# Dividing 128-column float products into two 64-column halves of the TensorE array in a recall block

## The chip, the cores and the metric

The program runs on one core of a Trainium2 chip. The metric is the device time of one execution in microseconds (us); the number compared is the median of several executions. The kernel uses five engines of the core: TensorE (PE, with its weight loads listed apart as PEld), VectorE (DVE), ScalarE (ACT), GpSimd (POOL) and SyncE (SP, here only DMA queues). Each engine works through its own instructions in order, and they wait for one another by semaphores.

## The reference

The program computes five layers over 8 batches of 1,056 tokens of 64 numbers: a patch embedding, an attention layer, a mixture of 16 experts, a recurrent "recall" layer and a mixture of 8 experts. The change touches the fourth alone. Cut to what matters it is, for every batch and token:

```python
def step(carry, v_prev):                       # v_prev: the token's 64 numbers; n = 256
    x_state, rho = carry
    x_t = 0.97 * x_state + relu(v_prev @ Dx.T)
    x_t = x_t / max(sum(abs(x_t)), 1e-12)
    a_star = einsum('bdn,bn->bd', rho, x_t)
    y_t = relu(_ln(a_star) @ Dy.T) * relu(x_t)
    v_star = _ln(y_t @ E.T)
    rho_t = 0.97 * rho + _ln(v_prev)[:, :, None] * x_t[:, None, :]
    return (x_t, rho_t), v_star
```

All of it is float32.

## The kernel before, in words

The recurrence is computed in tiles of 128 tokens: 8 full tiles and one of 32 for each batch. The block is `recall_answer_block`; `x_all` holds x with its 256 numbers along the partitions in two halves (`f` = 0, 1), tokens along the row. One loop counter n = 9 b + t runs through batch b and tile t on every engine (n from 0 to 89; the last 18 are the tail for what lags behind). What PE does in iteration n, in this order:

- `score(n+1)` (L2247): the 128x128 products of x with itself within a tile, two float products (one for each f) with 128 result columns, into `p_s`. VectorE multiplies it by the decay triangle (`mask`, L2426) into `pm`.
- `turn_x` (L2254): two transposes that bring x's tile to tokens-on-partitions; ScalarE copies them to `xr` (L2356).
- from batch 2 on, for the batch two back: `core` (L2300, 352 result columns, once in each of iterations 1 to 6), whose result VectorE turns into `yT` (`gate`, L2434; the next `core` waits for the gate before it); in iterations 7 and 8 `answer` (L2309), ten and eight products with 64 result columns.
- for the batch one back, in iterations 7, 8 and 0, `turn_la` (L2291): three transposes of the normalised rows `la`, which VectorE makes by `la_centre` (L2453) in iteration 5 and `la_scale` (L2460) in iteration 6.
- `weigh(n)`: the masked scores times the values (L2270, one product) and, from the second tile on, x times the state (L2274, two products), each with 64 result columns. It waits for `mask(n)` and for the state's copy.
- `keep_state` (L2282): two products with 64 result columns add the tile to the state in `p_r`; ScalarE copies it out (L2360).

Every float product stands in the trace as two pairs of a weight load and a matmul. VectorE runs, besides masks and gates, the scans of x for later batches (L1850, two for each batch: in iterations 4 and 6 of batch 0, in 4 and 7 of batch 1, and from then on in iteration 8 and in iteration 0 of the next batch), and the row statistics (L2440, L2445, L2148, L2156). GpSimd computes the inverse roots and adds the answer to `hid` (L2132 to L2140, about 8 us a batch). The block ends when all engines are through; the last piece there is GpSimd's L2140, and then the second expert stage starts, in which PE is the chain that sets the end.

In the tail (n from 72 on) the last two batches' `turn_la`, `core` and `answer` run, mixed with the routing (top-k) of the first batch of the next stage on VectorE.

Of the kernel before, what the change touches and what calls it, by code (L numbers as in the profile page):

```python
# [20 lines left out]
P = 128  # L21
B, C, T, V, D = 8, 64, 128, 64, 64
# [6 lines left out]
FULL = SEQ // P  # L29
CH = SEQ // 3  # L30
# [2128 lines left out]
def recall_answer_block(g, x_all, vn_all, rate_scr, feed, kb, trio, own, steps):  # L2159

    nc, hid, arg = g.nc, g.hid, g.arg
# [6 lines left out]
    la_turned, laT_ready, cored, gated, answered = (g.sem("k_" + n) for n in ("la_turned", "laT_ready", "cored", "gated", "answered"))  # L2168
    v_step = kb["v_step"]
    with ExitStack() as c:  # L2170
        sb = lambda n, s, d=F32: c.enter_context(nc.sbuf_tensor("k_" + n, s, d))
        ps = lambda n, s: c.enter_context(nc.psum_tensor("k_" + n, s, F32))
        tri, fade, pm, xr, state, a_sb, la, laT, yT, v_sb, dyT, eT = (
            kb[n] for n in ("tri", "fade", "pm", "xr", "state", "a_sb", "la", "laT", "yT", "v_sb", "dyT", "eT"))
# [5 lines left out]
        p_s, p_w = ps("p_s", [P, 2, 512]), ps("p_w", [P, 2, 512])  # L2180
        p_t, p_r = p_w[:, 0, :], p_w[:, 1, :]
# [4 lines left out]
        core_bank = lambda b, k: p_s[:, 0, :] if b >= B - 2 and k % 2 else p_y  # L2186
        AFTER = NT * B
        block = c.enter_context(nc.Block())
        rows_of = lambda t: P if t < FULL else TXT
        span = lambda t: slice(t * P, t * P + rows_of(t))  # L2190
        wide = lambda m: m.to_broadcast([P, NT, D])

        @block.sync
        def _(sp):
            _, load_biases, spread_out, spread_in, _ = sync_steps(sp)
            load_biases()
            load_levels(g, sp, kb, EARLY, B, late["scaled"], 1)
            send_rates(g, sp, kb, rate_scr, EARLY, B, 1)
            for b in range(EARLY, B):
                spread_rate(sp, kb, rate_scr, b)  # L2200
            sp.wait_ge(weighed, NT * 6)
            sp.wait_ge(gated, KW * 6)
            spread_out(0)
            spread_in(0, range(NC))
# [32 lines left out]
        @block.tensor  # L2237
        def _(pe):
            def score(n):
                b, t = divmod(n, NT)  # L2240
                if n >= 2:
                    pe.wait_ge(masked, n - 1)
                if t == 0:
                    pe.wait_ge(scanned, 2 * b + 2)
                x, rows = x_all[:, b, :, :], rows_of(t)
                for f in range(2):
                    last = nc.tensor.matmul(p_s[0:rows, n % 2, 0:rows], x[:, f, span(t)], x[:, f, span(t)], start=(f == 0), stop=(f == 1))  # L2247
                last.then_inc(scored, 1)

            def turn_x(b, t):  # L2250
                m = FULL * b + t
                pe.wait_ge(x_rows, m)
                for f in range(2):
                    last = nc.tensor.transpose(p_t[:, f * P:f * P + P], x_all[:, b, f, span(t)], g.eye[:])  # L2254
                last.then_inc(x_turned, 1)

            def weigh(n):
                b, t = divmod(n, NT)
                rows = rows_of(t)
                if t == 0:  # L2260
                    pe.wait_ge(a_kept, 2 * b)
                if n == FULL:
                    pe.wait_ge(kb["level"], LEVEL_STEPS + NC)
                    pe.wait_ge(kb["copied"], 2)
                if t == FULL:
                    pe.wait_ge(a_kept, 2 * b)
                    pe.wait_ge(v_kept, 2 * max(b - 2, 0))
                out = p_a[:, t, :] if t < FULL else p_last[0:TXT, 0:D]
                pe.wait_ge(masked, n + 1)
                last = nc.tensor.matmul(out, pm[0:rows, n % 2, 0:rows], vn_all[0:rows, b, t, :], start=True, stop=(t == 0))  # L2270
                if t:
                    pe.wait_ge(held, FULL * b + t)
                    for f in range(2):
                        last = nc.tensor.matmul(out, x_all[:, b, f, span(t)], state[:, f, :], start=False, stop=(f == 1))  # L2274
                last.then_inc(weighed, 1)

            def keep_state(b, t):
                m = FULL * b + t
                pe.wait_ge(x_rows, m + 1)
                pe.wait_ge(held, m)  # L2280
                for f in range(2):
                    last = nc.tensor.matmul(p_r[:, f * D:f * D + D], xr[:, m % 2, f * P:f * P + P], vn_all[:, b, t, :],  # L2282
                                            start=(t == 0 and f == 0), stop=(t == FULL - 1), skip_group_check=True)
                last.then_inc(stated, 1)

            def turn_la(b, k):
                pe.wait_ge(la_step, 2 * b + 2)
                pe.wait_ge(laT_ready, 3 * b + k)
                pe.wait_ge(gated, KW * b)
                for t in range(3 * k, 3 * k + 3):  # L2290
                    last = nc.tensor.transpose(p_y[0:D, t % 3 * P:t % 3 * P + P], la[:, t, :], g.eye[:])  # L2291
                last.then_inc(la_turned, 1)

            def core(b, k):
                f, a = divmod(k, NC)
                pe.wait_ge(laT_ready, 3 * b + 3)
                pe.wait_ge(gated, KW * b + (k if b < B - 2 else max(k - 1, 0)))
                if b >= B - 2:
                    pe.wait_ge(masked, NT * B)
                nc.tensor.matmul(core_bank(b, k)[:, 0:CH], dyT[:, f, :], laT[:, a * CH:a * CH + CH], start=True, stop=True).then_inc(cored, 1)  # L2300

            def answer(b, half):
                pe.wait_ge(gated, KW * b + KW)
                pe.wait_ge(v_kept, 2 * b)
                pe.wait_ge(a_kept, 2 * min(b + 2, B))
                for t in ((0, 1, 2, 3, 4), (5, 6, 7, 8))[half]:
                    out = p_v[:, t, :] if t < FULL else p_last[:, D:2 * D]
                    for f in range(2):
                        last = nc.tensor.matmul(out, yT[:, f, t * P:t * P + P], eT[:, f, :], start=(f == 0), stop=(f == 1))  # L2309
                last.then_inc(answered, 1)  # L2310

            _, turn_tokens, logits, turn_gates, _ = tensor_steps(pe)
            score(0)
            turn_x(0, 0)
            for n in range(NT * (B + 2)):
                b, t = divmod(n, NT)
                if n + 1 < NT * B:
                    score(n + 1)
                    if t + 1 != FULL:
                        turn_x(*divmod(n + 1, NT))  # L2320
                if n == 0:
                    pe.wait_ge(set_up, 4)
                    pe.wait_ge(own["w_copied"], 3)
                if b == B and t == 7:
                    for half in range(2):
                        answer(b - 2, half)
                if 1 <= b <= B and t >= 7:
                    turn_la(b - 1, t - 7)
                if b >= 2 and t == 0:
                    turn_la(b - 2, 2)  # L2330
                if n == AFTER + 8:
                    turn_gates(0)
                if b >= 2 and 1 <= t <= KW:
                    core(b - 2, t - 1)
                if b >= 2 and t >= 7 and b != B:
                    answer(b - 2, t - 7)
                if b < B:
                    weigh(n)
                    if t < FULL:
                        keep_state(b, t)  # L2340
                if AFTER + 2 <= n <= AFTER + 3:
                    if n == AFTER + 2:
                        pe.wait_ge(x_rows, FULL * B)
                        pe.wait_ge(held, FULL * B)
                    turn_tokens(0, n - AFTER - 2)
                if n == AFTER + 4:
                    logits(0)
# [195 lines left out]
def all_stages(g):  # L2543

    nc, arg = g.nc, g.arg
    with ExitStack() as c:
# [41 lines left out]
        with ExitStack() as c3:  # L2588
            buffers = recall_buffers(g, c3, c)
            trio = c3.enter_context(nc.psum_tensor("k_trio", [P, 3, 512], F32))  # L2590
            drive_block(g, x_all, feed, rate_scr, buffers, trio, own, steps)
            recall_answer_block(g, x_all, vn_all, rate_scr, feed, buffers, trio, own, steps)
# [39 lines left out]
```

## Time and profile before

| | us |
|---|---|
| median of 3 executions | 1810.58 |
| lowest, highest | 1808.53, 1818.72 |
| the profiled execution | 1824.75 |
| its span in the trace | 1822.9 |
| the recall block within it | 1325 to 1543 |
| PE busy, VectorE busy (whole span) | 1691.1, 1258.9 |
| granted TensorE clock, mean | 0.943 |

The trace is of one execution, some 14 us longer than the median. Busy times are unions of an engine's instructions, and the mean length of a matmul includes the time in which it drains, so the rate of PE is read from the distance between the starts of groups and not from the lengths. PEclk is the granted share of TensorE's full clock of 2.4 GHz; 0.50 is the lower level, 1.2 GHz.

### The profile page before, as it was taken

What the parts mean: (1) busy time and instruction counts of PE and PEld (TensorE: products, weight loads), DVE (VectorE), ACT (ScalarE), POOL (GpSimd) and SP (SyncE); (2) the same over time, 40 slices, a digit from 0 to 9 for tenths busy, and PEclk for the clock granted to TensorE, in tenths of its full rate; (3) what the DMA queues carried; (4) which work ended last, traced back from release to release, by engine and by line L of the source; (5) the groups of instructions that cost most, each with busy time, mean ns of one, the idle gap of its engine ahead of it and who ended that gap; (6) DMA issues with size and microseconds to landing.
All of it is one profiled execution on the core that took longest, in us unless ns stands there. A gap on an engine that the chain in (4) does not pass through costs nothing. (4 is left out here: it accounts for less than half of the span.)

```text
span 1822.9 us, 50042 instructions
## 1 busy us (share of the span) xinstructions
PE 1691.1 (93%) x20010; PEld 820.6 (45%) x20010; DVE 1258.9 (69%) x3153; ACT 1041.5 (57%) x1963; POOL 348.3 (19%) x325
## 2 busy tenths in 40 slices
PE   7978999999999999999999999999899997999999
PEld 3331222222222222222223655657488995566667
DVE  3459888888888888888722688886776664444432
ACT  1330777777777777777655555555533332666654
POOL 3212000000000000000100146655304434110000
PEclk9965999999999999999866999999999997999999
DMA  5741012121212112110113875563120002253350
GB/s 206 267 100 33 8 37 50 36 51 37 50 31 51 37 40 47 33 37 15 36 37 81 161 149 111 100 126 70 43 74 13 1 2 49 57 98 63 63 98 20
DMA packets 89587, 119.37 MB, mean 65 GB/s; under 512 B 31340, under 2 KB 72374, under 8 KB 87310
## 3 DMA queue, kind: packets, MB, share of 16 engines
q1 hardware_dynamic: 84874, 107.28, 27.0%
q0 software_dynamic: 2992, 8.44, 1.2%
q8 instruction: 161, 2.64, 0.6%
q10 hardware_dynamic: 1492, 0.46, 0.1%
q14 instruction: 68, 0.56, 0.1%
HBM read 97.29 MB, written 18.86 MB: 64 GB/s over the span
## 5 line engine op out<-in xcount | busy, mean ns | idle before, releaser
L870 ACT ACTIVATE b_prob<-b_p_s 128x512 f32<-128x512 f32 x1104 | 570.5, 599 | 273.8 <-PE b_p_s L1060 255.2
L893 DVE TENSOR_REDUCE b_m<-b_p_m 128x1 f32<-128x1024 f32 x512 | 604.0, 1219 | 85.1 <-PE b_p_s L1060 64.9
L1088 PE MATMUL b_p_o<-b_prob,v_all 128*9 128x512 f32 x2304 | 314.7, 630 | 1.0
L1486 ACT ACTIVATE d_hidden<-d_p_z 128x704 f32<-128x704 f32 x192 | 135.1, 755 | 98.6 <-PE d_p_z L1386 96.6
L1060 PE MATMUL b_p_s<-b_q,b_k 51*64 51x512 bf16 x1024 | 183.0, 420 | 2.4 <-ACT b_prob L870 2.4
L1486 ACT ACTIVATE n_hidden<-n_p_z 128x704 f32<-128x704 f32 x192 | 135.1, 755 | 84.6 <-PE n_p_z L1386 82.3
L1001 PE MATMUL b_p_m<-b_qk 48*64 48x512 bf16 x856 | 162.7, 441 | 21.8 <-ACT b_prob L870 5.4
L1060 PE MATMUL b_p_s<-b_qk 51*64 51x512 bf16 x1024 | 177.5, 401 | 2.2 <-ACT b_prob L870 2.2
L848 POOL DMA_DIRECT2D sum_scr<-b_sums x46 | 25.3, 550 | 718.5 <-ACT b_sums L860 631.8
L1402 PE MATMUL d_p_y<-d_hidden,d_w 64*64 64x352 f32 x1536 | 143.1, 460 | 9.0 <-DVE d_yT L1604 8.9
L1001 PE MATMUL b_p_m<-b_k,b_q 48*64 48x512 bf16 x800 | 137.2, 392 | 12.2 <-ACT b_prob L870 6.5
L1402 PE MATMUL n_p_y<-n_hidden,n_w 64*64 64x352 f32 x1536 | 142.1, 460 | 0.1
L1001 PEld LDWEIGHTS b_p_m<-b_qk 48*64 48x64 bf16 x856 | 38.4, 111 | 188.0 <-DVE b_m L893 123.2
L1001 PEld LDWEIGHTS b_p_m<-b_k,b_q 48*64 48x64 bf16 x800 | 35.1, 104 | 164.4 <-DVE b_m L893 98.6
L1402 PEld LDWEIGHTS d_p_y<-d_hidden,d_w 64*64 64x64 f32 x1536 | 74.3, 133 | 47.1 <-DVE d_yT L1604 19.2
L1386 PE MATMUL d_p_z<-d_xg,d_w 64*64 64x352 f32 x1024 | 94.0, 465 | 0.5 <-issue 0.5
L1386 PE MATMUL n_p_z<-n_xg,n_w 64*64 64x352 f32 x1024 | 92.6, 466 | 0.0
L1402 PEld LDWEIGHTS n_p_y<-n_hidden,n_w 64*64 64x64 f32 x1536 | 72.2, 133 | 39.8 <-DVE n_yT L1604 10.0
L1619 DVE TENSOR_TENSOR d_xg<-d_xd,d_c_wide 128x352 f32<-128x352 f32 x84 | 50.8, 648 | 47.6 <-PEq L674 31.8
L1604 DVE TENSOR_TENSOR n_yT<-n_yT,n_p_y 128x352 f32<-128x352 f32 x24 | 12.5, 522 | 95.0 <-ACT n_yT L1493 95.0
L1088 PEld LDWEIGHTS b_p_o<-b_prob,v_all 128*9 128x9 f32 x2304 | 37.7, 89 | 83.0 <-issue 54.9
L1001 PE MATMUL b_p_m<-b_k_head,b_q_head 48*64 48x512 bf16 x392 | 67.0, 405 | 6.3 <-ACT b_prob L870 4.6
(391 smaller groups left out, 2599.7 us busy)
## 6 DMA issues: line engine op xcount, KB each, us to landing
d_c_wide<-d_c_scr SPq DMA_DIRECT2D x40, 704.0 KB, 12.1
m_x_all<-n_c_scr SPq DMA_DIRECT2D x48, 352.0 KB, 7.9
xt<-in_x SPq DMA_DIRECT2D x16, 1024.0 KB, 10.6
sum_scr<-b_sums POOLq DMA_DIRECT2D x31, 256.0 KB, 2.4
qk_scr<-a_qk_part SPq DMA_DIRECT2D x24, 256.0 KB, 3.0
b_qk<-d_c_scr SPq DMA_DIRECT2D x8, 704.0 KB, 18.2
k_rate<-rate_scr SPq DMA_DIRECT2D x8, 528.0 KB, 4.4
b_qk<-qk_scr SPq DMA_DIRECT2D x56, 66.0 KB
```

The costliest lines, as they stand in the source:

```text
L848: pool.dma_start(g.sum_scr[b, p, :, a * WIDE:a * WIDE + w], sums[:, n % 2, 0:w]).then_inc(sum_sent[n % 2], 16)
L870: nc.scalar.activation(prob[:, U % PR_RING, 0:w], p_s[:, U % S_RING, 0:w], ACT.Exp, scale=float(D) ** -0.5).then_inc(exp_done, 1)
L893: nc.vector.tensor_reduce(m3[:, x, 0:1], p_m[:, s, :, :].rearrange("p k n -> p (k n)"), axis=AX.X, op=ALU.max).then_inc(rows_free, 1)
L1001: last = nc.tensor.matmul(out[e:e + 64, k, :], q[:, t * P + e:t * P + e + 64], keys[:, k * WIDE:k * WIDE + WIDE], start=True, stop=True)
L1060: last = nc.tensor.matmul(out[e:e + 64, :], k_st[s][r, q, jt * P + e:jt * P + e + 64], q_st[s][r, q, a * WIDE:a * WIDE + WIDE], start=True ...
L1088: last = nc.tensor.matmul(p_o[32 * i:32 * i + DH + 1, :], v[:, jt, p * QUAD + i, :], prob[:, slot, :], start=(jt == 0), stop=(jt == TILES[ ...
L1386: last = nc.tensor.matmul(own["p_z"][h * D:h * D + D, n % 2, q, 0:CH], w1[r, pr, cols:cols + D], own["xg"][n // HALVES % XR][r, :], start= ...
L1402: last = nc.tensor.matmul(own["p_y"][q * D:q * D + D, h, 0:CH], w2[r, 2 * pr + q, f, :], own["hidden"][r, n % HR, q, :], start=(k == 0), s ...
L1486: nc.scalar.activation(own["hidden"][:, n % HR, :, :], own["p_z"][:, n % 2, :, 0:CH], ACT.Relu).then_inc(relu_done, 1)
L1604: nc.vector.tensor_tensor(own["yT"][:, cols], own["yT"][:, cols], own["p_y"][:, 1, 0:CH], ALU.add).then_inc(sum_copied, 1)
L1619: nc.vector.tensor_tensor(own["xg"][j % XR], own["xd"][b % 3][:, a * CH:a * CH + CH], own["c_wide"][b % 2][a][:, pr, :], ALU.mult)\
```

## The change

Every float product whose weights have 128 columns is issued as two products of 64 weight columns, one for each column half of the array (result partitions 0 to 63 and 64 to 127), with the same moving data. The two transposes of `turn_x` become products with the identity, divided in the same way. The moving data, the waits and the increments stay; the increment is on the last product of the group. The small products of the 32-token tile and the transposes of `turn_la` are not divided.

```diff
+        halves_of = lambda rows: [(0, D), (D, P)] if rows == P else [(0, rows)]
...
                 for f in range(2):
-                    last = nc.tensor.matmul(p_s[0:rows, n % 2, 0:rows], x[:, f, span(t)], x[:, f, span(t)], start=(f == 0), stop=(f == 1))
+                    for lo, hi in halves_of(rows):
+                        last = nc.tensor.matmul(p_s[lo:hi, n % 2, 0:rows], x[:, f, t * P + lo:t * P + hi], x[:, f, span(t)], start=(f == 0), stop=(f == 1),
+                                                skip_group_check=True)
...
                 for f in range(2):
-                    last = nc.tensor.transpose(p_t[:, f * P:f * P + P], x_all[:, b, f, span(t)], g.eye[:])
+                    for lo, hi in halves_of(P):
+                        last = nc.tensor.matmul(p_t[lo:hi, f * P:f * P + P], x_all[:, b, f, t * P + lo:t * P + hi], g.eye[:, :], start=True, stop=True,
+                                                skip_group_check=True)
...
-                last = nc.tensor.matmul(out, pm[0:rows, n % 2, 0:rows], vn_all[0:rows, b, t, :], start=True, stop=(t == 0))
+                for lo, hi in halves_of(rows):
+                    last = nc.tensor.matmul(out[lo:hi, :], pm[0:rows, n % 2, lo:hi], vn_all[0:rows, b, t, :], start=True, stop=(t == 0), skip_group_check=True)
...
                     for f in range(2):
-                        last = nc.tensor.matmul(out, x_all[:, b, f, span(t)], state[:, f, :], start=False, stop=(f == 1))
+                        for lo, hi in halves_of(rows):
+                            last = nc.tensor.matmul(out[lo:hi, :], x_all[:, b, f, t * P + lo:t * P + hi], state[:, f, :], start=False, stop=(f == 1),
+                                                    skip_group_check=True)
...
                 for f in range(2):
-                    last = nc.tensor.matmul(p_r[:, f * D:f * D + D], xr[:, m % 2, f * P:f * P + P], vn_all[:, b, t, :],
-                                            start=(t == 0 and f == 0), stop=(t == FULL - 1), skip_group_check=True)
+                    for lo, hi in halves_of(P):
+                        last = nc.tensor.matmul(p_r[lo:hi, f * D:f * D + D], xr[:, m % 2, f * P + lo:f * P + hi], vn_all[:, b, t, :],
+                                                start=(t == 0 and f == 0), stop=(t == FULL - 1), skip_group_check=True)
...
-                nc.tensor.matmul(core_bank(b, k)[:, 0:CH], dyT[:, f, :], laT[:, a * CH:a * CH + CH], start=True, stop=True).then_inc(cored, 1)
+                for lo, hi in halves_of(P):
+                    last = nc.tensor.matmul(core_bank(b, k)[lo:hi, 0:CH], dyT[:, f, lo:hi], laT[:, a * CH:a * CH + CH], start=True, stop=True,
+                                            skip_group_check=True)
+                last.then_inc(cored, 1)
...
                     for f in range(2):
-                        last = nc.tensor.matmul(out, yT[:, f, t * P:t * P + P], eT[:, f, :], start=(f == 0), stop=(f == 1))
+                        for lo, hi in halves_of(P):
+                            last = nc.tensor.matmul(out[lo:hi, :], yT[:, f, t * P + lo:t * P + hi], eT[:, f, :], start=(f == 0), stop=(f == 1),
+                                                    skip_group_check=True)
```

## Rows read from the trace of the kernel before

**Rows 1.** The page: busy time of PE and VectorE over the span.
```profile
PE   1691.1 (93%) x20010; PEld 820.6 (45%) x20010; DVE 1258.9 (69%) x3153; ACT 1041.5 (57%) x1963; POOL 348.3 (19%) x325
...
PE 15%; DVE 0%; issue 0%; POOL 0%; POOLq 0%
```

**Rows 2.** Windows: stretch, its length, busy PE, PEld, DVE, ACT, POOL, PEclk, DMA.
```profile
1330.20:1340.40 10.20, 9.90 (x88) 9.56 (x88) 10.01 (x11) 3.41 (x11) 0.00 (x0) 1.00 0.08 14
1340.40:1354.60 14.20, 14.20 (x130) 13.74 (x130) 8.42 (x34) 5.79 (x18) 2.02 (x2) 1.00 0.31 117
1354.60:1365.50 10.90, 8.86 (x70) 7.74 (x71) 9.72 (x23) 4.39 (x13) 0.00 (x0) 1.00 0.24 78
1365.50:1380.20 14.70, 13.74 (x111) 12.51 (x109) 10.06 (x54) 3.36 (x10) 7.16 (x9) 1.00 0.05 19
...
1404.25:1414.93 10.68, 10.19 (x84) 9.31 (x84) 8.58 (x21) 4.41 (x13) 6.17 (x4) 1.00 0.01 2
1414.93:1428.40 13.47, 13.47 (x110) 12.46 (x109) 7.61 (x36) 3.35 (x10) 3.55 (x4) 1.00 0.01 1
...
1476.70:1503.60 26.90, 26.90 (x224) 25.08 (x223) 15.15 (x86) 8.88 (x26) 11.93 (x14) 1.00 0.01 2
...
1516.90:1524.50 7.60, 7.56 (x36) 7.56 (x37) 3.05 (x14) 0.00 (x0) 5.53 (x5) 0.50 0.01 2
```

**Rows 3.** Timeline of PE: a steady step, and one answer (start, length, group).
```profile
1446.20 0.33 PE L2270 MATMUL k_p_a<-v_all,k_pm 128*128 128x64 f32 x2
1446.37 0.61 PE L2274 MATMUL k_p_a<-k_state,m_x_all 128*128 128x64 f32 x4
1446.81 0.61 PE L2282 MATMUL k_p_w<-v_all,k_xr 128*128 128x64 f32 x4
1447.26 0.66 PE L2247 MATMUL k_p_s<-m_x_all 128*128 128x128 f32 x4
1447.76 0.38 PE L2254 MATMUL k_p_w<-eye,m_x_all 128*128 128x128 f32 x2
1447.98 0.76 PE L2300 MATMUL k_trio<-k_laT,k_dyT 128*128 128x352 f32 x2
1448.57 0.33 PE L2270 MATMUL k_p_a<-v_all,k_pm 128*128 128x64 f32 x2
...
1454.71 1.90 PE L2309 MATMUL k_trio<-k_eT,k_yT 128*128 128x64 f32 x16
1456.54 0.29 PE L2270 MATMUL k_trio<-v_all,k_pm 32*32 32x64 f32 x2
```

**Rows 4.** PE in tiles elsewhere: timeline of the expert stage; the page's attention group.
```profile
1590.81 0.64 PE L1374 MATMUL n_p_w<-eye,n_yT 64*64 64x64 f32 x31
1591.28 0.46 PE L1386 MATMUL n_p_z<-n_w_raw,n_w 64*64 64x352 f32 x1
...
L1088 PE MATMUL b_p_o<-b_prob,v_all 128*9 128x512 f32 x2304 | 314.7, 630 | 1.0
```

**Rows 5.** Timeline: VectorE's chain around a batch's first tiles, and the core behind it.
```profile
1454.37 0.29 DVE L2426 TENSOR_TENSOR k_pm<-k_p_s,k_tri 128x128 f32<-128x128 f32 x1 [3.50 <-PE k_p_s L2247]
1454.58 3.17 DVE L1850 TENSOR_TENSOR_SCAN m_x_all<-m_x_all,k_rate 128x1056 f32<-128x1056 f32 x1
...
1461.91 0.51 DVE L2434 SCALAR_TENSOR_TENSOR k_yT<-k_trio,m_x_all 128x352 f32<-128x352 f32 x1
...
1462.57 0.83 PE L2300 MATMUL k_trio<-k_laT,k_dyT 128*128 128x352 f32 x2 [0.49 <-DVE k_yT L2434]
```

**Rows 6.** Timeline: `la_scale` on VectorE and `turn_la` on PE.
```profile
1449.21 0.75 DVE L2460 TENSOR_TENSOR k_la<-k_la,k_a_mv 128x576 f32<-128x576 f32 x1
...
1450.02 0.52 PE L2291 MATMUL k_trio<-eye,k_la 128*64 128x128 f32 x3
```

**Rows 7.** Timeline of the tail: the long answer, and GpSimd's last addition.
```profile
1516.94 7.95 PE L2309 MATMUL k_trio<-k_eT,k_yT 128*128 128x64 f32 x36 [4.89 <-DVE k_yT L2434]
...
1541.67 1.40 POOL L2140 TENSOR_TENSOR hid<-hid,k_v_sb 128x576 f32<-128x576 f32 x1
```

## The prediction

> **What bounds the kernel now.** I read the page first. PE is busy for 93% of the span and makes nearly all of the chain that ended last [rows 1], but a busy PE says little, because its matmuls overlap. So I went to the windows of the recall block, cut at the tiles of the loop [rows 2]. The reader is to see two kinds of stretch. From tile 2 to tile 7 of a batch (13.47 us) PE never idles while VectorE is at 7.61: PE sets the pace. From tile 7 to tile 2 of the next batch (10.68 us) PE is busy 10.19, and VectorE, with two scans, 8.58: there both are near their limit. The two make a batch of 24.15 us. Batches 0 and 1 have stretches in which VectorE fills 10.01 of 10.20 and 9.72 of 10.90 us.
>
> Then the timeline of one PE step [rows 3]: 1446.20 to 1448.57, 2.37 us. Its 2 + 4 + 4 records with 64 result columns start 0.111 us apart (four of L2282 in 0.45), and so do the two transposes (0.22). The core's two records with 352 columns take 0.295 each, 0.84 ns a column. By that rate 64 columns would stream in 0.054, so the 64-column records are not bound by streaming but by loading 128 weight columns, 0.111 each. Score, with 128 columns, streams in 0.107: load and stream are level.
>
> **The change, part by part.** What decides is the price of a 64-column load and matmul when the other half of the array works beside it. The nearest row is the expert stage, which uses four 64x64 tiles: between 1590.81 and 1591.28 it starts 32 float records of 64 result columns (31 in the group, one beside it), 0.47 / 8 = 0.059 us for four [rows 4]. Two of those tiles share the same rows and differ in the column half; were their loads one after the other, a round would need twice 0.056, the half of 0.111. For all 128 rows the trace shows column tiles in the attention: 2,304 records of 512 columns in 314.7 us of busy time, 0.137 each, where 512 columns at 0.84 ns stream in 0.43: three to four run side by side. So I take 0.059 for one record on each half.
>
> A rule speaks against that. Loads overlap there only across row groups, and two column halves of a 128-row product share theirs: the Trainium skill, "TensorE: Matmul & The Clock Gate", Part 3 (packing small matmuls), says that a load overlaps with in-flight matmuls only when the row group differs. The trace disagrees for the expert stage's column halves, by the 0.059 above, and shows nothing for halves of 128 rows with 64-column loads. By the rule the sum below would be a loss (first rival).
>
> - A product with 64 result columns is two records now, 0.222, and then four on two halves, 2 x 0.059 = 0.117: it saves 0.105. Bounds: 0 if loads queue (4 x 0.056), 0.115 if only streaming counts.
> - Score: 4 records of 0.111 become 8, two at a time, 4 x 0.107 to 0.111: nothing. It lies on PE's own path, so if the halves did not overlap it would cost 0.43.
> - Core: 2 x 0.295 become 4, two at a time: nothing; 0.59 if they did not overlap, which the attention row makes unlikely.
> - turn_x: two transposes of one record each, 0.22, become eight records of 128 columns, 4 x 0.111 = 0.44: it costs 0.22. Bounds 0.21 to 0.64, the latter if the halves do not overlap.
> - No wait is added. The increments stay on the last product of each group.
>
> A full step has five short products and one turn: 5 x 0.105 - 0.22 = 0.30 saved of 2.37. An answer tile has two: 0.21. Were PE the bound everywhere, a batch would save 56 x 0.105 - 8 x 0.22 = 4.1 us, and eight batches 33. But not all of it is PE's.
>
> Steady batch, tile 7 to tile 2. VectorE runs one unbroken chain here: the mask at 1454.37 starts when the first score of the next batch is there, then come scan, statistics, mask, scan, statistics, mask and the gate of 1461.91, and the second core waits 0.49 for that gate [rows 5]. From mask to core, 8.2 us, nothing gets faster. Only what precedes the mask does: weigh and keep of tile 7, 0.53. So 0.53 is saved here, where PE alone would give 1.3 and the 0.49.
>
> Tile 2 to tile 7. Four full steps save 1.2. In the last interval weigh, keep and the five-tile answer save 0.53 + 1.05. But turn_la waits for la_scale, which ends at 1449.96, and starts at 1450.02 [rows 6]: no slack. la_scale stands behind the gate of the last core, and PE then reaches turn_la 0.53 sooner after that core. So I take 0.5 off: 1.1. Together 2.3.
>
> What I checked behind these: the state's copy (L2360, 0.28) has score, turn, core and the first weigh as cover, 1.6 us; a core follows the last by 2.06, while core and gate need about 1.4; VectorE would be busy 16.2 of 21.3 us a batch.
>
> | stretch | saved, us |
> |---|---|
> | 1325 to 1330, two steps, partly waiting for VectorE | 0.5 |
> | 1330.2 to 1340.4, VectorE full | 0 |
> | 1340.4 to 1354.6: PE-bound, -2.2, less 0.6 hidden by a scan | 1.6 |
> | 1354.6 to 1365.5, scans, VectorE chain | 0 |
> | 1365.5 to 1380.2: three steps 0.9, last interval 1.1 | 2.0 |
> | 1380.2 to 1390.8 | 0.5 |
> | three steady batches to 1463.2, 0.53 + 2.3 each | 8.4 |
> | 1463.2 to 1476.7 | 2.3 |
> | 1476.7 to 1503.6: no scans; intervals 1.15 - 0.2 + 0.1 + 5 x 0.30 + 1.1 + 1.37, less 0.3 as VectorE has routing work | 4.7 |
> | the long answer of the tail | 3.4 |
> | the last answer | 0 |
>
> The long answer [rows 7] runs at a granted clock of 0.50 [rows 2], the 1.2 GHz level, after PE sat idle for VectorE's routing: 36 records take 7.6 us. In halves at the same clock: 18 products x 2 x 0.117 = 4.2. It is on the path: turn_la and the six cores of batch 7 follow, then their gates, then GpSimd's 6 us, which end the block at 1543.1. The last answer (1536.4 to 1540.6) lies beside GpSimd's work, so its 2 us are hidden.
>
> Sum: 23.4 us. The stages behind the block are bound by PE and start when it ends, so they shift. Against the profiled execution's 1824.75 us that is 1801.4; the same 23.4 off the median of 1810.58 gives 1787.2.
>
> **The rivals.**
>
> *Loads of the two halves queue* (the other side). If the halves of 128 rows load one after the other, a short product needs 4 x 0.056 = 0.22 as now, and turn_x still costs 0.22 on 64 tiles. Some 50 of the 64 lie where PE sets the pace: +11 us, 1822. It decides as soon as a short product saves less than 64 x 0.22 / 448 = 0.032 us. For it: with 128 rows the trace has column tiles only with loads of 9 columns, so nothing there shows a 64-column load beside another. Against it: the four-tile row, in which two column halves share rows. This is what the page's rule comes to.
>
> *Half an overlap.* A round of 0.085 instead of 0.059 gives 0.05 a short product: 22 - 14 = 8 us on PE, and some of it where VectorE binds: 4 to 8 us, 1804 to 1806.
>
> *VectorE takes it.* If its in-order queue (masks behind scans, statistics and la_centre) binds in the 13.47 us stretch too, four steps save half and the tail's answer alone is safe: 12 to 15 us, 1797. For it: at 21 us a batch VectorE is at 76%, and several of its chains had slack below 1 us. Against: in each step it now idles 0.9 us in two waits.
>
> *The clock comes back sooner.* The half clock now lasts from about 1514 to 1534. With halves the long answer streams without pause; if the clock rises before the transposes and cores, these get up to 3 us shorter, and 6 us in all: 1783. The transfers of `m_x_all`, which run until about 1542 and start behind the same answer, let no more through.
>
> **How the numbers follow.** A measurement of this kernel tells a change from none at about 0.5%, 9 us. Forecast as summed (1780 to 1795): 0.58. Clock sooner or nearer to the full 33 us (1774 to 1780): 0.09. VectorE (1795 to 1801): 0.13. Half an overlap: 0.10. Loads queue: 0.10. Faster by over 0.5% (below 1801.5): the first three, 0.80; within: half an overlap, 0.10; slower: 0.10. The range of 1778 to 1805 takes in the bounds of the main case, VectorE and most of the half overlap, and leaves out the loss and the best end; the main case's own is 1780 to 1795.
>
> **What would show it.** In the new timeline: eight records of L2282 between group starts 0.23 apart (0.45 if loads queue, and turn_x at 0.44 either way); a steady step of 2.06; batches of 21.3 us with PE waiting about 1.3 us for the gate in tile 1 and 0.5 for la_scale before turn_la; the long answer 4.2 us long. If the steps are right and the sum is not, the next place is VectorE's chains. What would break it outright: a gap on PE at each change between full and 32-token tiles that is now hidden, or the two halves of a full-height product not running together.

## The result, and the profile after

The changed kernel takes 1791.84 us (median of 4, 1780.75 to 1795.65), the kernel before in the same rounds 1814.38 (median of 4, 1808.53 to 1818.72): a ratio of 0.9874, interval 0.984 to 0.9907. Forecast were 1787 us (1778 to 1805) and a ratio of 1787.2 / 1810.58 = 0.987; the kernel before had itself moved from 1810.58 to 1814.38 with the fourth execution. The profiled execution took 1795.65 us, its span 1793.8.

Single executions of one kernel differ by about 1%, and much of that arises ahead of the recall block, where no code differs. So kernels are compared by **the block**: from the start of the first score's first matmul to the start of the first matmul of the next stage (L1336). It began at 1325.0 before and at 1320.4 after; what follows it takes 279.3 and 280.2 us. Between, it took 218.60 us before and 193.27 after: 25.3 saved, where the prediction's sum was 23.4.

The page of the kernel after, busy times, and the two groups of the expert stage's chain that still end last; against [rows 1] PE has 1,632 more records and 39 us less of busy time, 32 of it in the block (202.12 us before).

```profile
PE 1652.3 (92%) x21642; PEld 780.3 (43%) x21642; DVE 1249.6 (70%) x3153; ACT 1041.6 (58%) x1963; POOL 355.6 (20%) x325
...
PE n_p_z L1386 7%; PE n_p_y L1402 7%; PE n_p_w L1336 1%; PE n_p_w L1374 0%; PE n_p_w L1345 0%; PE n_p_y L1365 0%; PE n_p_z L1415 0%; DVE hid L1593 0%; PE n_p_w L1354 0%; PE n_p_w L1355 0%; POOL n_yT L1306 0%; POOLq L2170 0%
```

The windows after (columns as in [rows 2]): the whole block; then the stretches that were 14.70, 13.47, 10.68 and 26.90 long [rows 2]; last the long answer, 7.60 before.

```profile
1320.40:1513.67 193.27, 170.14 (x3198) 140.46 (x3198) 135.74 (x561) 68.01 (x194) 87.95 (x72) 0.97 0.13 34
...
1359.93:1371.78 11.85, 11.10 (x230) 9.52 (x227) 8.90 (x52) 3.36 (x10) 7.24 (x7) 1.00 0.07 21
...
1402.19:1413.53 11.34, 10.88 (x230) 9.52 (x227) 7.30 (x36) 3.35 (x10) 2.89 (x4) 1.00 0.01 3
1413.53:1423.33 9.80, 9.23 (x175) 7.48 (x173) 8.32 (x21) 4.53 (x13) 8.77 (x4) 1.00 0.01 3
...
1455.80:1478.37 22.57, 22.10 (x456) 18.57 (x452) 14.07 (x80) 9.00 (x26) 10.62 (x12) 1.00 0.01 4
...
1491.98:1496.02 4.04, 4.04 (x73) 3.92 (x73) 3.01 (x14) 0.00 (x0) 2.24 (x2) 0.50 0.01 4
```

A steady batch went from 24.15 to 11.34 + 9.80 = 21.14 us. The window that was 26.90 long ends 0.20 behind the last tile's first product, so 22.57 is to be set against 26.70. The long answer has twice the records, and from its first to its last start it takes 3.79 instead of 7.52 us, at the same granted clock of 0.50.

The timeline of PE after: a steady step, then the end of interval 6, interval 7, and the core in tile 1.

```profile
1427.42 0.31 PE L2276 MATMUL k_p_a<-v_all,k_pm 128*64 128x64 f32 x4
1427.54 0.43 PE L2281 MATMUL k_p_a<-k_state,m_x_all 128*64 128x64 f32 x8
1427.77 0.43 PE L2291 MATMUL k_p_w<-v_all,k_xr 128*64 128x64 f32 x8
1428.01 0.64 PE L2249 MATMUL k_p_s<-m_x_all 128*64 128x128 f32 x8
1428.44 0.64 PE L2258 MATMUL k_p_w<-eye,m_x_all 128*64 128x128 f32 x8
1428.88 0.79 PE L2310 MATMUL k_trio<-k_laT,k_dyT 128*64 128x352 f32 x4
1429.47 0.31 PE L2276 MATMUL k_p_a<-v_all,k_pm 128*64 128x64 f32 x4
...
1433.00 0.52 PE L2300 MATMUL k_trio<-eye,k_la 128*64 128x128 f32 x3 [0.46 <-DVE k_la L2474]
1433.45 1.39 PE L2322 MATMUL k_trio<-k_eT,k_yT 128*64 128x64 f32 x40
...
1435.69 0.61 PE L2258 MATMUL k_p_w<-eye,m_x_all 128*64 128x128 f32 x8
1436.23 0.52 PE L2300 MATMUL k_trio<-eye,k_la 128*64 128x128 f32 x3
1436.67 1.15 PE L2322 MATMUL k_trio<-k_eT,k_yT 128*64 128x64 f32 x32
1437.75 0.29 PE L2276 MATMUL k_trio<-v_all,k_pm 32*32 32x64 f32 x2
...
1443.85 0.81 PE L2310 MATMUL k_trio<-k_laT,k_dyT 128*64 128x352 f32 x4 [0.57 <-DVE k_yT L2448]
```

Start to start, the eight records of L2281 take 0.23 us where four took 0.44, score 0.43 (0.50 before), the turn 0.44 (0.22 before), the core 0.59 as before: 2.05 for the step, against 2.37 [rows 3]. (Line numbers moved with the edit: `score` is L2249, `turn_x` L2258, `weigh` L2276 and L2281, `keep_state` L2291, `turn_la` L2300, `core` L2310, `answer` L2322.) PE now waits at two places of a batch, 0.46 for `la_scale` and 0.57 for a gate.

The timeline of VectorE after, in the same batch (against [rows 5, 6]):

```profile
1432.20 0.75 DVE L2474 TENSOR_TENSOR k_la<-k_la,k_a_mv 128x576 f32<-128x576 f32 x1
...
1435.91 0.29 DVE L2440 TENSOR_TENSOR k_pm<-k_p_s,k_tri 128x128 f32<-128x128 f32 x1 [2.26 <-PE k_p_s L2249]
1436.11 3.17 DVE L1850 TENSOR_TENSOR_SCAN m_x_all<-m_x_all,k_rate 128x1056 f32<-128x1056 f32 x1
...
1439.89 2.57 DVE L1850 TENSOR_TENSOR_SCAN m_x_all<-m_x_all,k_rate 128x1056 f32<-128x1056 f32 x1
...
1443.20 0.51 DVE L2448 SCALAR_TENSOR_TENSOR k_yT<-k_trio,m_x_all 128x352 f32<-128x352 f32 x1
```

### The profile page after: what moved, and what is told of

Same layout as the page of the kernel before. It is cut to its first block and busy times, and to the rows that moved or that the text cites. A ratio compares the mean times of both kernels' runs of the same rounds, so it can differ in the third digit from the quotient of the medians.

```text
span 1793.8 us, 53306 instructions
## 1 busy us (share of the span) xinstructions
PE 1652.3 (92%) x21642; PEld 780.3 (43%) x21642; DVE 1249.6 (70%) x3153; ACT 1041.6 (58%) x1963; POOL 355.6 (20%) x325
## 5 line engine op out<-in xcount | busy, mean ns | idle before, releaser
L1088 PE MATMUL b_p_o<-b_prob,v_all 128*9 128x512 f32 x2304 | 310.9, 623 | 1.0
L1001 PE MATMUL b_p_m<-b_qk 48*64 48x512 bf16 x856 | 162.7, 442 | 21.8 <-ACT b_prob L870 5.4
L848 POOL DMA_DIRECT2D sum_scr<-b_sums x46 | 25.3, 550 | 718.4 <-ACT b_sums L860 696.8
```

The lines of the kernel that those rows point to most:

```text
L848: pool.dma_start(g.sum_scr[b, p, :, a * WIDE:a * WIDE + w], sums[:, n % 2, 0:w]).then_inc(sum_sent[n % 2], 16)
L1001: last = nc.tensor.matmul(out[e:e + 64, k, :], q[:, t * P + e:t * P + e + 64], keys[:, k * WIDE:k * WIDE + WIDE], start=True, stop=True)
L1088: last = nc.tensor.matmul(p_o[32 * i:32 * i + DH + 1, :], v[:, jt, p * QUAD + i, :], prob[:, slot, :], start=(jt == 0), stop=(jt == TILES[ ...
```

## The experiments

Blocks are read from each kernel's own trace. A step is one interval with a core and no wait; a batch is a steady one; the tail runs from the long answer's start to the next stage.

| kernel | block | step | batch | tail |
|---|---|---|---|---|
| before | 218.6 | 2.37 | 24.15 | 26.7 |
| after | 193.3 | 2.05 | 21.14 | 21.7 |
| e3, one half left out | 191.8 | 2.05 | 21.12 | 21.9 |
| e4, one half twice | 227.3 | 2.63 | 26.33 | 22.8 |
| e5, halves in the outer loop | 193.0 | 2.05 | 21.15 | 21.8 |
| e1, transposes kept | 194.9 | 2.13 | 21.48 | 22.7 |
| e8, score and core whole | 219.7 | 2.75 | 24.97 | 22.9 |
| e9, only short products divided | 195.9 | 2.19 | 21.71 | 20.8 |
| e6, only the turn divided | 246.7 | 2.94 | 27.79 | 26.3 |
| e7, `la_scale` ahead of the gate | 188.8 | 2.05 | 19.82 | 20.1 |
| e10, e7 and statistics later | 189.3 | 2.05 | 19.82 | 21.5 |
| e12, GpSimd's wide pieces narrow | 185.4 | 2.05 | 20.36 | 16.8 |
| e11, only the long answer divided | 214.0 | 2.37 | 24.15 | 21.7 |

Each experiment but e10 was executed once, so it is judged by its trace. A block is good to about 1 us: from its start to the first tile of batch 1 after, e3, e7, e10 and e12 run the same code, and this takes 18.2, 17.5, 19.5, 19.3 and 17.5 us. Steps and batches repeat to 0.02 where the work is the same.

### Do the halves run side by side? (e3, e4, e5)

In e3 and e4 the short products (those with 64 result columns) of the full tiles, from batch 1 on, use another list of halves: e3 leaves the upper half out, e4 computes the lower one twice, so neither has the upper half's results. e5 only changes the order.

```diff
+        short_of = lambda rows, b: halves_of(rows) if b == 0 or rows != P else [(0, D)]              # e3
+        short_of = lambda rows, b: halves_of(rows) if b == 0 or rows != P else [(0, D), (0, D)]      # e4
...
-                for f in range(2):
-                    for lo, hi in halves_of(rows):
+                for lo, hi in halves_of(rows):                                                       # e5
+                    for f in range(2):
```

> Leaves out, from batch 1 on, the upper half (result partitions 64 to 127) of every product with 64 result columns (weigh, keep_state, answer); score, core and turn_x are as in the changed kernel. Theory (the two halves load and work side by side, a round of two costs what one costs, 0.058 us): PE's steps do not change, a steady step stays at 2.05 us, and the block from the first score to the first matmul of the next stage stays at 193 us, within 2. Rival (the halves share something, and a half alone would be quicker than 0.058 a record): a short product falls below 0.117, a step below 2.0, and the block to 185 or less.

> From batch 1 on, the upper half of every product with 64 result columns is replaced by a second copy of the lower one, so the same number of records all go to one column half (the upper half's results are not computed). This makes the rival of the prediction, loads that queue, by construction. Theory: four records one after the other, 4 x 0.058 = 0.23 us a short product, so a steady step is 2.05 + 5 x 0.117 = 2.64 us, the long answer of the tail goes from 4.1 to 8.2 us, and the block from 193 to 230 to 240 us. Rival (what counts is the number of records or their issue, not where they go): step and block as in the changed kernel, 2.05 and 193 us.

> The changed kernel with the order turned round: both products (f = 0, 1) of the lower half are issued first, then both of the upper half, in score, turn_x, weigh's state part, keep_state and answer. The same work, four records to one half in a row instead of two. Theory 1 (matmuls start in program order, so two records overlap only where the half changes): a group of eight records takes some 6 to 7 rounds where it took 4, a steady step is 2.5 to 2.9 us instead of 2.05, the block 215 us or more. Theory 2 (each half has its own queue and the order is free): 2.05 and 193 us.

The timeline of PE in e3, then in e4:

```profile
1419.84 0.28 PE L2277 MATMUL k_p_a<-v_all,k_pm 128*64 128x64 f32 x2
1419.96 0.40 PE L2282 MATMUL k_p_a<-k_state,m_x_all 128*64 128x64 f32 x4
```

```profile
1449.81 0.39 PE L2277 MATMUL k_p_a<-v_all,k_pm 128*64 128x64 f32 x4
1450.04 0.63 PE L2282 MATMUL k_p_a<-k_state,m_x_all 128*64 128x64 f32 x8
1450.51 0.57 PE L2292 MATMUL k_p_w<-v_all,k_xr 128*64 128x64 f32 x7
1450.86 0.32 PE L2250 MATMUL k_p_s<-m_x_all 128*64 128x128 f32 x1
1450.92 0.22 PE L2292 MATMUL k_p_w<-v_all,k_xr 128*64 128x64 f32 x1
```

With half the records e3's groups start as far apart as after, 0.12 for the first: the second half is free. (Of the 1.4 us by which its block is shorter, 1.3 lie ahead of tile 7 of batch 1, where blocks vary by chance.) With the same number of records, all on one half, e4's take 0.23 and 0.47, and its block is 227.3 us, 9 slower than before: it is the first rival, built. (That is less than the 230 to 240 expected; the step, 2.63, is as expected, the long answer takes 6.27 from first to last start and not 8.2.) So the number of records costs nothing as long as they are spread over both halves: which half each goes to decides. e5 puts two records of one half in a row in every divided group but the first and the core, and neither step nor block moves: the order within a group doesn't matter. In e4 the records even start out of order: the first record of `score` (L2250, 1450.86) starts ahead of the last of `keep_state` (L2292, 1450.92), which is issued before it. The trace doesn't name the halves, but in e4 only the upper one has nothing in line before `score`. Each half is served as if it had its own queue.

For halves of 128 rows a pair of loads takes 0.058 us, where one after the other takes 0.117, as in e4. The rule that the prediction weighed ("TensorE: Matmul & The Clock Gate", Part 3, in the Trainium skill: loads overlap only across row groups) doesn't hold there. The Trainium skill's "TensorEngine Tiling (Array Packing)", Key Properties, says that different tiles can load and multiply in parallel, and e3 agrees.

### What the parts that gain nothing are for (e1, e8, e9, e6)

e1 takes back the turn alone; e8 score and core; e9 all three, so that only the short products are divided; e6 is the kernel before with only the turn divided.

```diff
# e1, e9
-                    for lo, hi in halves_of(P):
-                        last = nc.tensor.matmul(p_t[lo:hi, f * P:f * P + P], x_all[:, b, f, t * P + lo:t * P + hi], g.eye[:, :], start=True, stop=True,
-                                                skip_group_check=True)
+                    last = nc.tensor.transpose(p_t[:, f * P:f * P + P], x_all[:, b, f, span(t)], g.eye[:])
# e8, e9 (the core likewise)
-                    for lo, hi in halves_of(rows):
-                        last = nc.tensor.matmul(p_s[lo:hi, n % 2, 0:rows], x[:, f, t * P + lo:t * P + hi], x[:, f, span(t)], start=(f == 0), stop=(f == 1),
-                                                skip_group_check=True)
+                    last = nc.tensor.matmul(p_s[0:rows, n % 2, 0:rows], x[:, f, span(t)], x[:, f, span(t)], start=(f == 0), stop=(f == 1))
```

> The changed kernel, but turn_x is again two transposes with 128 weight columns. Theory 1 (a change between weights of 128 and of 64 columns is free, so only the 0.22 us of the turn counts): a steady step falls from 2.05 to 1.83 us, a batch from 21.1 to about 19.9 (the VectorE chain keeps its part), the block from 193 to 185 us. Theory 2 (the array drains at each change of width, as its loads can't be taken ahead): two changes a step cost 0.1 to 0.2 us each, and the step is 2.0 to 2.2 us, the block 190 to 197 us; gaps then stand before the load of turn_x and the load behind it.

> The changed kernel, but score and core are again single products with 128 weight columns; weigh, keep_state, turn_x and answer stay in halves. By streaming alone nothing is gained or lost by dividing these two. Theory 1 (each change of width costs 0.15): four changes a step instead of none, a steady step of 2.05 + 0.6 = 2.65 us, the block 222 to 230 us. Theory 2 (the change of width costs only beside transposes): 2.05 and 193 us.

> Only the products with 64 result columns (weigh, keep_state, answer) are in halves; score, turn_x (as transposes) and core keep 128 weight columns, as in the kernel before. A step has two changes of width, since score, turn and core follow one another. By 0.15 to 0.175 each: 2.37 - 0.53 + 0.30 to 0.35 = 2.14 to 2.19 us a steady step, the block about 197 us. Rival (changes of width cost only beside transposes or only in the four-change kernel's order): 1.83 us and 185.

> The kernel before, with turn_x alone changed (products with the identity, in halves); all other products keep 128 weight columns. Theory: the turn costs 0.22 us more, and each of its two changes of width about 0.15 (the whole-transposes run showed 0.30 for two), so a steady step goes from 2.37 to 2.9 us and the block from 218.6 to about 242 us. Rival (the turn alone counts): 2.59 us and 229.

The weight loads of e1 around the transposes, and the timeline of PE in e8, one step:

```profile
1441.07 0.45 PEld L2249 LDWEIGHTS k_p_s<-m_x_all 128*64 128x64 f32 x8
1441.69 0.20 PEld L2257 LDWEIGHTS k_p_w<-eye,m_x_all 128*128 128x128 f32 x2 [0.17 <-issue]
1442.06 0.20 PEld L2308 LDWEIGHTS k_trio<-k_laT,k_dyT 128*64 128x64 f32 x4 [0.17 <-issue]
```

```profile
1452.46 0.40 PE L2289 MATMUL k_p_w<-v_all,k_xr 128*64 128x64 f32 x8
1452.79 0.71 PE L2248 MATMUL k_p_s<-m_x_all 128*128 128x128 f32 x4
1453.43 0.66 PE L2256 MATMUL k_p_w<-eye,m_x_all 128*64 128x128 f32 x8
1454.02 0.86 PE L2307 MATMUL k_trio<-k_laT,k_dyT 128*128 128x352 f32 x2
1454.81 0.34 PE L2274 MATMUL k_p_a<-v_all,k_pm 128*64 128x64 f32 x4
```

In e1 each passage between products in halves and whole ones leaves the load side idle for 0.17 us. e1 has two in a step: its turn is 0.22 shorter and its step 0.08 longer, so the two cost 0.30, 0.15 each. e8 has four: 2.75 against 2.05, 0.175 each. e9 has two: by the prediction's terms 2.37 - 5 x 0.105 = 1.845 and 2.19 is measured, 0.17 each. e6 has two as well: 2.37 + 0.22 leaves 0.35. With four passages e8 loses the whole gain (219.7 us, below the 222 to 230 expected, though its step is longer than the 2.65 expected). e6, whose turn is by itself only 0.22 dearer, is 28 us slower than before (246.7 us where 242 was expected). Dividing score, turn and core, which save nothing of their own, is what keeps the step free of passages; between e9 and after that is worth 0.14 a step and 2.6 us of block. It is the smaller part: e9, with two passages a step, still has 22.7 of the 25.3 us. The Trainium skill's "TensorEngine Tiling (Array Packing)", Key Properties, says that a change of tiling mode drains TensorE; the traces agree and put it at 0.15 to 0.175 us.

The number of columns in a record's name doesn't decide what is a passage. `turn_la` was left as transposes; its records stand as 128*64, like the halves beside it, and still there are passages. The load side after, then before:

```profile
1476.84 0.25 PEld L2300 LDWEIGHTS k_trio<-eye,k_la 128*64 128x64 f32 x3
...
1477.29 1.01 PEld L2322 LDWEIGHTS k_trio<-k_eT,k_yT 128*64 128x64 f32 x32 [0.20 <-issue]
```

```profile
1450.02 0.25 PEld L2291 LDWEIGHTS k_trio<-eye,k_la 128*64 128x64 f32 x3
1450.26 0.64 PEld L2309 LDWEIGHTS k_trio<-k_eT,k_yT 128*128 128x128 f32 x5
```

After, a divided answer follows and there is a gap of 0.20; before, a whole one follows and there is none. In e9 (turn whole, answers divided) the gap stands only behind `turn_la`, 0.20; in e6 (turn divided, answers whole) only ahead of it, 0.17. So these transposes of 64 columns go with the whole products. In starts, from the turn to `turn_la` it is now 0.54 us where from the turn to a core it is 0.44, and from `turn_la` to the answer 0.44 where it was 0.32 before (1454.39 to 1454.71). That is 0.10 to 0.12 for a passage, and of the six in a batch five are not hidden by the wait for `la_scale`: an estimate of 0.5 to 0.6 us a batch that after still pays. Whether dividing `turn_la` too would save it wasn't tried.

### Where PE still waits (e7, e10, e12)

e7 puts `la_scale` ahead of the gate in VectorE's iteration 6; e10 also moves the row statistics of tiles 4 to 8 from iteration 0 to 1; e12 cuts GpSimd's three wide pieces of `answer_add` to one element per partition, so it leaves out most of the answer's normalising and adding.

```diff
+                if 1 <= b <= B and t == 6:        # e7, e10: here, ahead of the gate
+                    la_scale(b - 1)
...
-                    if t == 0:                    # e10: these rows with t == 1
-                        a_rows(b - 1, (4, 5, 6, 7, 8))
...
-    nc.gpsimd.tensor_tensor(v, v, wide(v_mv[:, :, 0:1]), ALU.subtract).then_inc(v_step, 1)
+    nc.gpsimd.tensor_tensor(v[:, 0, 0:1], v[:, 0, 0:1], v_mv[:, 0, 0:1], ALU.subtract).then_inc(v_step, 1)   # e12
```

> The changed kernel, with VectorE's la_scale issued ahead of the gate of the same iteration instead of behind it; nothing else. Theory (turn_la waits for la_scale alone, which stands behind the last core's gate): the wait of 0.46 us before the first turn_la of a batch goes, the gate is hardly later, and with 7 such places the block is 3 us shorter, 190 us. Rival (the wait only moves: the later gate holds up the answer behind turn_la): block 193 us.

> As the run before, and the second half of the row statistics (a_rows of tiles 4 to 8, 0.7 us) moved from iteration 0 to iteration 1, behind the gate. Theory (in iteration 1 PE waits 0.57 us for the gate, at the end of VectorE's chain of masks, scans and statistics): that wait goes too, in five batches, 2.5 to 3 us; the block is about 187 us and the median 0.3% below the changed kernel's. Rival (something else is late at the same place, so the wait gets another name): block 190 us.

> The changed kernel; GpSimd's three wide operations on the answer (centre, scale, add to the hidden state, 128x576 each) are cut down to one column, so the answer isn't normalised and added. Theory (a scan that VectorE starts while a wide GpSimd operation runs has to wait for its end, and the chain from the first mask to the gate is that much longer): all scans from batch 2 on take 2.35 us instead of 3.17 and 2.57, PE's wait of 0.57 us for the gate in tile 1 goes, and a steady batch is 20.6 us instead of 21.1. Rival (scans are slow for another reason, such as ScalarE or PE reading beside them): scans and batch as in the changed kernel.

e7 took 1.32 us off a batch where 0.46 had been waited for: 0.57 in tile 6, and 0.76 in tile 1, where the wait for the gate is gone. GpSimd's timeline after, then VectorE and GpSimd in e7, show where the rest came from:

```profile
1435.90 1.17 POOL L2136 TENSOR_TENSOR k_v_sb<-k_v_sb,k_v_mv 128x576 f32<-128x576 f32 x1
1437.15 3.10 POOL L2138 TENSOR_TENSOR k_v_sb<-k_v_sb,k_v_mv 128x576 f32<-128x576 f32 x1
```

```profile
1403.66 2.35 DVE L1850 TENSOR_TENSOR_SCAN m_x_all<-m_x_all,k_rate 128x1056 f32<-128x1056 f32 x1
...
1406.78 2.40 DVE L1850 TENSOR_TENSOR_SCAN m_x_all<-m_x_all,k_rate 128x1056 f32<-128x1056 f32 x1
```

```profile
1403.70 3.27 POOL L2136 TENSOR_TENSOR k_v_sb<-k_v_sb,k_v_mv 128x576 f32<-128x576 f32 x1
1407.05 3.10 POOL L2138 TENSOR_TENSOR k_v_sb<-k_v_sb,k_v_mv 128x576 f32<-128x576 f32 x1
```

After, GpSimd's piece starts at 1435.90, the scan at 1436.11: GpSimd takes its 1.17 and the scan 3.17. In e7 the scan starts 0.04 ahead: it takes 2.35 and GpSimd's piece 3.27. Whoever comes second is longer. e12 takes GpSimd's data away. The timelines of VectorE and of GpSimd in e12, same batch:

```profile
1441.25 2.35 DVE L1850 TENSOR_TENSOR_SCAN m_x_all<-m_x_all,k_rate 128x1056 f32<-128x1056 f32 x1
...
1444.37 2.35 DVE L1850 TENSOR_TENSOR_SCAN m_x_all<-m_x_all,k_rate 128x1056 f32<-128x1056 f32 x1
```

```profile
1441.04 0.19 POOL L2136 TENSOR_TENSOR k_v_sb<-k_v_sb,k_v_mv 128x1 f32<-128x1 f32 x1
1441.31 2.27 POOL L2138 TENSOR_TENSOR k_v_sb<-k_v_sb,k_v_mv 128x1 f32<-128x1 f32 x1
1443.66 0.19 POOL L2140 TENSOR_TENSOR hid<-hid,k_v_sb 128x1 f32<-128x1 f32 x1
```

Both scans take 2.35, and the batch, 20.36, is 0.78 shorter by it. The same piece of one element per partition takes 0.19 alone and 2.27 when it starts 0.06 after a scan: it ends with the scan. That is waiting, not slower work.

The Trainium skill's "SBUF — State Buffer", section "SBUF: two separate sides", says that a port pair is shared by the two engines as an exclusive lock, that a VectorE operation with two SBUF inputs takes it, and that the second to come blocks. The scan has two such inputs, and these timelines agree. In e10 the second move gave nothing on top of e7: with the scans short, the wait in tile 1 was already gone. So my expectation of 187 was wrong; the block is near the rival's 190, but not for the rival's reason, as nothing else was late there. e10 was also timed: 1779.39 us (median of 6), ratio to the kernel before 0.9815 (0.9782 to 0.9847), where the change by itself gave 0.9874 (0.984 to 0.9907); the two intervals just touch, so how much of that is e10's own is read from the block, 4 us.

### The tail (e11)

```diff
+                        for lo, hi in ([(0, D), (D, P)] if b == B - 2 else [(0, P)]):
+                            last = nc.tensor.matmul(out[lo:hi, :], yT[:, f, t * P + lo:t * P + hi], eT[:, f, :], start=(f == 0), stop=(f == 1),
```

> The kernel before, with only the answers of batch 6 (the long one of the tail) in halves. Theory (the records of the long answer stream without pause in halves, and the clock is back at its upper level sooner): long answer 3.8 us instead of 7.5, the half clock there 7 to 14 us instead of 20.5, and from the long answer to the next stage 21.7 to 22.8 us instead of 26.7. Rival (the clock's return has nothing to do with it): half clock 17 to 21 us and 23 us.

The timeline of PE in e11 at the long answer, and the windows from there (columns as in [rows 2]):

```profile
1499.77 4.11 PE L2310 MATMUL k_trio<-k_eT,k_yT 128*64 128x64 f32 x72 [4.88 <-DVE k_yT L2436]
```

```profile
1497.00:1503.80 6.80, 4.03 (x72) 3.92 (x72) 5.60 (x39) 0.00 (x0) 2.24 (x2) 0.50 0.01 2
1503.80:1514.00 10.20, 7.71 (x33) 3.74 (x31) 3.92 (x15) 3.29 (x8) 4.50 (x4) 0.83 0.40 67
```

One answer of 18 products, divided by itself, gives the tail 5.0 of its 5.0 us. First to last start it takes 3.79 instead of 7.52; and the clock was at 0.50 for 20.5 us before, from 1514.0, but here for 6.8 and once more for 3.4, as after. The block as a whole saved 4.6: ahead of the long answer, where the code is that of before, it is 0.4 longer by chance.

## Why the prediction was right, step by step

| stretch | predicted | measured |
|---|---|---|
| start to tile 7 of batch 0 | 0.5 | 0.4 |
| to tile 7 of batch 1 | 1.6 | 0.4 |
| the next 10.6 us | 0 | 0.2 |
| 1365.5 to 1380.2 | 2.0 | 2.8 |
| 1380.2 to 1390.8 | 0.5 | 1.3 |
| three steady batches | 8.4 | 9.0 |
| 1463.2 to 1476.7 | 2.3 | 2.1 |
| 1476.7 to 1503.6 | 4.7 | 4.1 |
| the long answer and behind it | 3.4 | 4.9 |
| sum (rows rounded) | 23.4 | 25.3 |

The mechanism and the sum both held, but the sum is nearer than its terms, which is luck: 1.2 and 0.6 us too much in two rows stand against 0.8, 0.8, 0.6 and 1.5 too little in four others. Two slips change nothing: three times 2.83 is 8.5 and not 8.4, and the price at which the first rival decides is 0.031 and not 0.032.

- *Short product at 0.117, from the four-tile row.* Confirmed: pairs start 0.058 apart; e3 and e4 exclude the rivals "loads queue" and "half an overlap".
- *Score and core for nothing, turn +0.22.* Core and turn to 0.01. From the start of the short products to that of score the step saves 0.47, where five times 0.105 is 0.53, and score, put at nothing, takes 0.43 instead of 0.50. The step is 2.05, forecast 2.07.
- *Tile 2 to tile 7, 2.3.* Measured 2.13 in the steady batch (13.47 to 11.34), with the wait of 0.46 before `turn_la` where 0.5 was taken off. The four steps give 1.30 for 1.2, the last interval 0.83 for 1.1: the passage behind `turn_la`, which the prediction has nowhere, takes 0.10 of that.
- *"From mask to core nothing gets faster", 0.53.* This step was a little off: 0.88. The mask starts 0.58 sooner, as said, but from mask to core it is 7.94 instead of 8.20, because the second scan takes 2.57 instead of 2.82 beside GpSimd's pieces (e7 and e12 show that length to be GpSimd's doing). The wait for the gate is 0.57, not 1.3: VectorE's chain is shorter, and PE's own work there fell from 10.19 to 9.23, by 0.96 and not 1.3, as it now has four passages around `turn_la`.
- *1340.4 to 1354.6, 1.6.* The largest shortfall, 0.4 for 1.6. One wait, 0.69 for the mask behind a scan ahead of batch 1's first score, had been allowed for with 0.6. Not allowed for is a stop of 0.59 in tile 6 of batch 1 (1347.6 to 1348.2), in the middle of the records of `weigh`. The profile names nothing that it waits for. It isn't `la_scale`, which ends at 1348.47, before `turn_la` starts at 1349.03, and e7, where `la_scale` comes sooner, has the stop too (0.46). What it is stays open.
- *1380.2 to 1390.8, 0.5.* 1.3 were saved, and much of it is luck: before, the first scan there started 0.05 behind a GpSimd piece and took 3.33 us; after, it misses that piece and takes 2.35. Why 1365.5 to 1380.2 gave 2.8 is known in part: `turn_la` waited 0.79 for `la_scale` there before, and 0.46 after.
- *The long answer at half clock, 4.2 for 7.6, 3.4 saved.* Near: 3.79 for 7.52 from first to last start, 3.73 saved; "the clock comes back sooner" came on top and goes with the other 1.2 of the tail's 5.0, of at most 3 that the rival gave it. Why the lower clock lasts 6.8 us in one run and 20.5 in another stays open: after as in e3, e4, e5, e7, e9, e10, e11 and e12 it was first 6.8, in e1 and e8 13.7, in e6, whose answers are whole, 17.1.
- *VectorE takes it.* No: in the PE-bound stretch it is at 7.30 of 11.34, and PE waits there only the 0.46 for `la_scale`.
- *What follows the block shifts.* It does: 279.3 and 280.2 us.

## What to carry to other kernels

A float product whose result is narrower than its 128 weight columns pays for the load, and two column halves load side by side: look for records that start further apart than their moving columns stream. Count the passages between divided and whole products: four in a step took the whole gain back, two took 2.6 of 25.3 us, and dividing neighbours that gain nothing by themselves removes them. When a stretch is freed, read next which small operation of the other engines starts first: moving one operation of 0.75 us gave 4.5 us of block.

## What was not expected of the hardware

- A passage between products in column halves and whole ones costs 0.15 to 0.175 us in the steady step (e1, e6, e8, e9), and 0.10 to 0.12 around `turn_la`. Transposes of 64 columns count as whole: before, with whole products around them, they show no gap; after, with halves around them, they do.
- A scan on VectorE that starts 0.2 us after a GpSimd piece of 1.17 us is 0.82 us longer (3.17 against 2.35); a GpSimd piece that starts just after a scan takes 3.27 instead of 1.17, and one of a single element per partition 2.27 instead of 0.19.
- The order of records between the two halves makes no difference (e5: 193.0 against 193.3 us), and in e4 a record starts ahead of one issued before it (1450.86 and 1450.92), by the edit one for the other half.
- In tile 6 of batch 1 PE stops for 0.46 to 0.73 us in the middle of a group after and in e5, e7, e10 and e12, and not in the others; nothing in the profile explains it.
